# A decoder layer on one core: the second half's x is split before it is turned, and turned by transposing DMAs

## The reference, cut to what matters

```python
def _L0_attn_ref(u, ...):                       # u = x, axes l (16), b (256), d (512)
    xn = _layernorm(u, ln_gamma, ln_beta)
    up = jnp.einsum('lbd,ed->lbe', xn, W_in) + b_in          # e: 3 * 512
    uc = short causal convolution over l, 3 taps, of up
    x0, x1, v = jnp.split(uc, 3, axis=1)
    v = v * x1
    y = long convolution of v over l with k, + v * conv_bias
    y = y * x0
    return jnp.einsum('bld,ed->ble', y, W_out)
x = _layernorm(x + _L0_attn_ref(x, ...))
```

## Time and profile before

| what | us |
|---|---|
| three runs, median (lowest to highest) | 1064.82 (1059.51 to 1065.6) |
| the profiled execution's own time | 1063.69 |
| its span, first to last instruction | 1061.9 |
| TensorE busy | 1006.2 (95%) |
| VectorE busy | 799.3 (75%) |
| ScalarE busy | 599.9 (56%) |
| GpSimd busy | 552.7 (52%) |
| first half's output steps on TensorE | 182.33 to 246.17 |
| second half's slots, steps, and the end of the part | 246.17 to about 459 |

### The profile page before, as it was taken

The page is one execution under the profiler, slowest core; times in us unless marked ns, Lnnn a source line. Parts: engine busy times, 40 slices in busy tenths (PEclk is TensorE's granted clock), DMA queues, the critical chain, the costliest instruction groups (busy, mean ns, idle before and its releaser), DMA issues.

```text
span 1061.9 us, 14827 instructions
## 1 busy us (share of the span) xinstructions
PE 1006.2 (95%) x4679; PEld 602.9 (57%) x4679; DVE 799.3 (75%) x1509; ACT 599.9 (56%) x728; POOL 552.7 (52%) x886
## 2 busy tenths in 40 slices
PE   3899999999999999978999999999999999999985
PEld 2455545544445555456666666666666666666641
DVE  7967975786475567657888888888888888888862
ACT  5655544112566558114666666767576767676664
POOL 5320310221000004269787887878787878787861
PEclk9999999999999999989999999999999999999998
DMA  9323655456475777441444544444444444444334
GB/s 322 61 60 120 203 152 163 145 165 194 162 227 189 241 259 255 141 143 51 105 98 113 105 113 108 115 106 117 104 117 105 109 114 101 122 99 114 76 64 91
DMA packets 178220, 144.65 MB, mean 136 GB/s; under 512 B 99988, under 2 KB 132792, under 8 KB 176120
## 3 DMA queue, kind: packets, MB, share of 16 engines
q1 hardware_dynamic: 178168, 144.00, 49.3%
HBM read 89.29 MB, written 33.70 MB: 116 GB/s over the span
## 4 chain that ended last, share of the span: by engine, by line
PE 50%; DVE 2%; POOL 1%; ACT 1%; DMA 1%; issue 1%; POOLq 0%; DVEq 0%; ACTq 0%
PE conv_bank L1398 28%; PE hq_bank L1421 9%; PE ff_bank L1442 5%; PE back_bank L1442 5%; PE back_bank L1412 1%; PE back_bank L1381 1%; PE ctx_bank L1369 1%; DMA hq_t<-hq_int 0%; POOL sum L1742 0%; DVE z L1607 0%; DVE g_max L1674 0%; POOL sum L1744 0%; ACT g L1546 0%; DMA xq_t<-xq_int 0%; ACT hq_f L1507 0%
## 5 line engine op out<-in xcount | busy, mean ns | idle before, releaser
L1742 POOL TENSOR_TENSOR sum<-z 128x640 f32<-128x640 f32 x128 | 198.2, 1549 | 11.6 <-DVE z L1619 9.6
L837 DVE SCALAR_TENSOR_TENSOR conv_all<-u,taps,conv_all 128x1024 f32<-128x1024 f32 x92 | 122.4, 1331 | 93.2 <-ACT conv_all L708 91.4
L1398 PE MATMUL conv_bank<-block_diag 128*128 128x288 f32 x628 | 167.8, 411 | 1.8 <-DVE z L1619 1.8
L1398 PE MATMUL conv_bank<-kv,block_diag 128*128 128x288 f32 x640 | 168.6, 406 | 0.9 <-DVE z L1619 0.8
L1398 PEld LDWEIGHTS conv_bank<-kv,block_diag 128*128 128x128 f32 x640 | 117.8, 190 | 31.6 <-DVE z L1619 1.8
L1398 PEld LDWEIGHTS conv_bank<-block_diag 128*128 128x128 f32 x628 | 117.3, 193 | 32.4 <-DVE z L1619 2.2
L1421 PE MATMUL hq_bank<-x_lo,hq_t 128*128 128x512 f16 x512 | 122.2, 382 | 4.7 <-DMA hq_t<-hq_int 4.7
L1674 DVE TENSOR_REDUCE g_max<-g 128x1 f32<-128x512 f32 x128 | 85.8, 673 | 41.5 <-ACT g L1546 41.5
L700 ACT ACTIVATE u<-slot_bank,bias,unscale 128x1024 f32<-128x1024 f32 x46 | 55.4, 1204 | 108.9 <-PE slot_bank L509 88.6
L1744 POOL TENSOR_TENSOR sum<-sum 128x320 f32<-128x320 f32 x128 | 111.3, 869 | 10.0
L1607 DVE TENSOR_TENSOR z<-conv_bank,qx 128x512 f32<-128x512 f32 x128 | 88.0, 687 | 34.2 <-PE conv_bank L1398 24.6
(11 more groups left out here) (181 smaller groups left out, 1676.2 us busy)
## 6 DMA issues: line engine op xcount, KB each, us to landing
x_quad<-in_w SPq DMA_DIRECT2D x10, 1024.0 KB, 8.3
v_scratch<-conv_all SPq DMA_DIRECT2D x16, 512.0 KB, 3.5
c_scratch<-v_tok SPq DMA_DIRECT2D x8, 1024.0 KB, 5.3
y<-c_scratch SPq DMA_DIRECT2D x8, 1024.0 KB, 4.9
res<-in_x SPq DMA_DIRECT2D x32, 256.0 KB, 2.9
x_scratch<-res SPq DMA_DIRECT2D x32, 256.0 KB, 3.1
block_diag<-in_ctx SPq DMA_DIRECT2D x32, 256.0 KB, 3.7
block_diag<-ssm_scratch SPq DMA_DIRECT2D x32, 256.0 KB, 3.7
```

The source lines that it names most:

```text
L837: ins = nc.vector.scalar_tensor_tensor(out=acc, in0=(u_first[kind] if n < 3 else u)[:, t0 + tap:t0 + tap + T // 2, :].rearrange("p t b -> ...
L1398: last = nc.tensor.matmul(view(conv_bank[tb % 2][:, hh, :], 0, (ROW64, T // 2), (1, PAIRS)), toep[:, head.buf, (tb - sb_) * P:(tb - sb_ + ...
L1742: nc.gpsimd.tensor_tensor(sum2[:, :, :], z[:, b, :, 0:half], z[:, b, :, half:2 * half], ALU.add).then_inc(sum2_done, 1)
```

## The change

For the second half only, TensorE's 64 transposes (with 16 ScalarE copies and 16 VectorE subtractions out of PSUM) go. In their place, ScalarE casts a normalized quad to its float16 high part (`make_hi`, 128x2048 in one instruction), VectorE subtracts it from the quad to a float16 rest (`make_lo`, likewise), both still with the batch on the partitions and in an order of (block of 128 features, time, feature). The two lie side by side in a tile that is free by then (`conv[X1]`, `conv[V]`, `v_tok`, `conv[X0]` for quads 0 to 3). SyncE then issues two transposing DMAs a quad (`turn_halves`), each of 128x2048 float16, which write `x_hi` and `x_lo`, whose layout is now quad by quad. Slots 0 and 1 wait for these DMAs. `make_hi` stands after slots 20 and 23 for quads 0 and 1 and after the slots for quads 2 and 3; `make_lo` after slot 22 and in output steps 2, 9 and 12; the transposing DMAs behind the stores of output steps 0, 4, 10 and 13. The loads of x into `x_quad` wait for `make_lo` in place of the transposes. The first half works as before.

```diff
+        half_rows = [view(tile, 0, (1, T * P)).bitcast(F16) for tile in (conv[X1], conv[V], v_tok[:, :], conv[X0])]
+        def token_half(q, low):
+            return view(half_rows[q], low * QUAD * D, (1, QUAD * D))
+        def by_chunk(ap, step_dc, step_t):
+            return view(ap, 0, (step_dc, DC), (step_t, QUAD), (1, P))
...
-        QUAD_AT = {1: 0, 4: 1, 9: 2, 13: 3}
+        HI_AT = {20: 0, 23: 1}
+        LO_AT = {22: 0}
+        LATE_LO_AT = {2: 1, 9: 2, 12: 3}
+        TURN_X_AT = {0: 0, 4: 1, 10: 2, 13: 3}
...
@@ load_quad (SyncE)
-                        sp.wait_ge(x_turned, DC * (Q - 1))
+                        sp.wait_ge(lo_made, Q - NQ - 1)
...
+                def turn_halves(q):
+                    if q == 0:
+                        sp.wait_ge(slot_full, NSLOT)
+                    for low, (made, x) in enumerate(((hi_made, x_hi), (lo_made, x_lo))):
+                        sp.wait_ge(made, q + 1)
+                        sp.dma_start_transpose(view(x[:, q, :, :], 0, (P, DC * QUAD), (1, P)), token_half(q, low)).then_inc(halves_turned[q], 16)
...
                         store_res(R)
+                        if hf + 1 < HALF and t in TURN_X_AT:
+                            turn_halves(TURN_X_AT[t])
                         if hf + 1 < HALF and t in LOAD_QUAD_AT:
...
@@ slot (TensorE)
-                        elif hf > 0 and s < 2 and j < 2:
-                            pe.wait_ge(made, DC * (NQ * hf + 2 * (s + 1)))
+                        elif hf > 0 and s < 2 and j == 0:
+                            for q in group:
+                                pe.wait_ge(halves_turned[2 * pr + q], 2 * 16)
...
-                        if hf + 1 < HALF and t in QUAD_AT:
-                            turn_quad(NQ * (hf + 1) + QUAD_AT[t])
...
+                def make_hi(q):                                  # ScalarE
+                    act.wait_ge(x_normed, q + 1)
+                    if q == 0:
+                        act.wait_ge(vx_done, 2 * DC)
+                    elif q == 1:
+                        act.wait_ge(v_stored, 2 * 16 * DC)
+                    elif q == 2:
+                        act.wait_ge(c_stored, 16 * DC)
+                    else:
+                        act.wait_ge(y_done, 4 * DC)
+                    src = quad_buf(NQ + q)[:, :, :].rearrange("p t d -> p (t d)")
+                    nc.scalar.copy(by_chunk(token_half(q, 0), QUAD * P, P), by_chunk(src, P, D)).then_inc(hi_made, 1)
...
+                def make_lo(q):                                  # VectorE
+                    dve.wait_ge(hi_made, q + 1)
+                    src = quad_buf(NQ + q)[:, :, :].rearrange("p t d -> p (t d)")
+                    hi, lo = (by_chunk(token_half(q, low), QUAD * P, P) for low in range(2))
+                    nc.vector.tensor_tensor(lo, by_chunk(src, P, D), hi, ALU.subtract).then_inc(lo_made, 1)
...
-                        if more and t in QUAD_AT:
-                            split_lo(nxt + QUAD_AT[t])
+                        if more and t in LATE_LO_AT:
+                            make_lo(LATE_LO_AT[t])
```

More of the change, by code:

```diff
@@ L88, in hyena_block @@
         shift = sb("shift", [P, NQ, QUAD])
-        x_hi, x_lo = w["x_hi"], w["x_lo"]
+        x_hi, x_lo = (view(w[name][:, :, :], 0, (DC * QUAD * P, NQ), (QUAD * P, DC), (1, QUAD * P)) for name in ("x_hi", "x_lo"))
         u = sb("u", [P, T + TAPS - 1, P])
@@ L144, in hyena_block @@
         x_lo_done = sem("x_lo_done")
+        hi_made = sem("hi_made")
+        lo_made = sem("lo_made")
+        halves_turned = [sem(f"halves_turned{q}") for q in range(NQ)]
         u_zeroed = sem("u_zeroed")
@@ L457, in _ @@
             def _(pe):
[L458 to L464, removed]
                 def turn_quad(Q):
@@ L512, in slot, with convolve @@
                         last.then_inc(slot_full, 1)
-                def convolve(hf, cc, others=(), quad=None):
+                def convolve(hf, cc, others=()):
                     first = chain_counts(hf, cc)
@@ L521, in convolve @@
                     for k in range(4):
-                        if quad is not None:
-                            pe.wait_ge(x_lo_done, DC * quad + k + 1)
-                        elif not others:
+                        if not others:
                             pe.wait_ge(ch_copied, first - 4 + k + 1)
@@ L639, in _ @@
                         for cc in pieces_after(s):
-                            others, quad = (), None
+                            others = ()
                             if hf == 0 and cc < DC - 1:
                                 others = [(w_lo_done, KINDS * (cc + 2))] + [(wout_done, DC)] * (cc == 0)
-                            elif hf > 0 and cc == 0:
-                                quad = NQ * (hf + 1) - 1
                             if hf == 0 and cc == 0:
@@ L650, in _ @@
                                 pe.wait_ge(mean_made, 1)
-                            convolve(hf, cc, others, quad)
+                            convolve(hf, cc, others)
                     for t in range(PARTIAL):
@@ L784, in _ @@
                             copy_conv(hf, cc)
+                        if hf == 0 and s in HI_AT:
+                            make_hi(HI_AT[s])
                         if hf + 1 == HALF and s in SQUARE_AT:
@@ L789, in _ @@
                     if hf + 1 < HALF:
-                        for q in range(NQ):
-                            split_hi(NQ * (hf + 1) + q)
+                        make_hi(2)
+                        make_hi(3)
                 for i in range(2 * PARTS):
@@ L1001, in _ @@
                             norm_quad(nxt + QUAD_NORM_AT[s])
+                        if more and s in LO_AT:
+                            make_lo(LO_AT[s])
                         if not more and s == TOTAL_AT:
```

18 lines of the change are left out of this document (6 added, 12 removed).

## The result

The changed kernel took 1077.08 us (median of 4 runs, 1076.14 to 1078.82), the kernel before 1064.99 in the same runs: a ratio of 1.012, 95% interval 1.0089 to 1.015. The change costs 12.1 us. The forecast was 1085, the range 1068 to 1098: right in sign and mechanism, with the size overestimated by two thirds. The 1077 lies inside the forecast's own narrower range (1077 to 1093) only at its very edge.

The account below looks back on a forecast made before the run. TensorE was busiest, but SyncE's loop of landing, load and store was taken to have no slack. Slot 4 +17.8 us and clock +2.7 gave 20.5 us on 1063.69, 1084.2, stated as 1085; range 1068 to 1098.

Parts of the forecast that it names:

- The removal is worth nothing by itself: SyncE's output-step loop: a turn takes about 3.45 us, as much as TensorE's step, despite 8.8 us of removed TensorE work.
- The casts and subtractions are free: Four ScalarE casts and four VectorE subtractions: all eight taken at nothing; at most the first pair costs 1.9 + 2.5 us.
- A half takes 3.4 us of the transfer engines: Each 512 KB transposing transfer occupies all 16 engines 3.4 us, from 153 GB/s; bounds 2.8 us and 5 us.
- rival 4: Transposes slower beside loads: at 5 us a half, slot 4 about +32, total 1098 with the clock's share; chance 0.16.
- Rival 3: A transpose as fast as a plain transfer: 1.6 us a half, slot 4 at +4.7, total 1068; chance 0.05.
- 2.5 us of SyncE for a pair: SyncE's queue: issuing one pair of transposing transfers holds SyncE 2.5 us, from 1.25 us for one issue.
- The loop, step by step: SyncE's loop: pairs behind steps 0, 4 and 10 delay it by +4.3, +9.7 and +13.7 us.
- The last pair sets slot 1: Second half's slot 1 waits for step 13's pair: starts at 271.5 in place of 251.35.
- The weights' load behind the loop no longer shows by itself: Before slot 4: this load, behind the last pair, frees slot 4 at 286.9, against 287.0 from slot 1; earlier stall 2.14 us.
- The clock, +2.7: TensorE after idling 11 us before slot 1: granted clock at half costs 2.7 us; bounds 0 and twice that.
- Nothing gives it back: Behind slot 4: no delay is recovered, TensorE's waits there all being under 2 us until the second part.
- Rival 1: Only the wait on the last pair costs, the loop keeps its times: slot 4 +4.1, total 1068; chance 0.15.

Follow-up runs that it names:

- Experiment 1: Changed kernel without its eight transposing transfers and the second half's waits for them, so no transposes at all: 1064.2 us, ratio 0.9981 to the kernel before.
- experiment 4: Changed kernel with all eight transposing transfers issued by ScalarE in place of SyncE, each once its subtraction is done: 1073.5 us, ratio 1.0072.
- experiment 2: Changed kernel without the transposing pairs of output steps 0 and 4 and the wait for them: 1070.3 us, ratio 1.0053.
- experiment 3: Changed kernel with the last transposing pair behind the store of output step 12 in place of 13: 1073.7 us, ratio 1.0082.
- experiment 10: Changed kernel with 64 unread fill matmuls on TensorE between slots 0 and 1 of the second half: 1078.7 us, ratio 1.014.
- experiment 8: Changed kernel with stores first, quad loads, statistics, normalization and subtractions moved earlier, pairs behind steps 1, 3, 6 and 9: 1063.2 us, ratio 0.9983.
- experiment 11: As experiment 8, but each pair's two transposes put behind two neighbouring steps in place of one: 1052.7 us, ratio 0.989.
- (5): Changed kernel with one swap in SyncE's loop, the step's store issued before the residual load: 1074.9 us, ratio 1.0101.
- (12): Changed kernel with each pair's second transpose moved behind the next step's store, loads still first: 1076.0 us, ratio 1.0097.

## Why the prediction was right, and where its sizes were off

- **The removal is worth nothing by itself** ("this loop has no slack to give"): right, and stronger than I put it. Experiment 1 shows 8.8 us of TensorE's work gone and 0.3 us between the medians, at most 4 by the interval.
- **The casts and subtractions are free:** right. A cast took 1.9 us, a subtraction 2.29 us, and experiment 1, which keeps them, is no slower than the kernel before.
- **A half takes 3.4 us of the transfer engines:** this term was mis-sized, the main miss. I took the row of 153 GB/s, of a transfer of half the size. Landings of the three sizes say 187 GB/s, 2.8 us a half, the value that I had kept as the fast bound; the stretch in which a half moves alone says 219 GB/s, 2.4 us. The same walk with 2.8 us gives +12.8 us to slot 4 (the prediction's "+14" was a slip, and so was rival 4's "about +32", which comes to +30.5), with the clock 15.5, against 14.6 measured: this one term is 5.0 of the 8.3 us by which the sum was too high. The figure of the Trainium skill, page "Advanced Engine Details and Errata", section X-Bar Transpose (TRN2), an expected 350 to 400 GB/s, is not reached here. Rival 3, which stood on a transfer that fast, is out: at 1.6 us a half a landing would take some 3.4 us, and none was under 4.3.
- **2.5 us of SyncE for a pair:** wrong, it is 4.7 to 5.9. No cost of it by itself is seen: experiment 4 frees SyncE of it and the loop is hardly shorter.
- **The loop, step by step:** forecast +4.3, +9.7, +13.7 at the loads at 203.69, 227.14 and 244.91; measured, with the 2.1 us of the later start taken off, +3.1, +4.9 and +8.5. The pairs' data explain 3.9 of the last gap of 5.2 us: from the first half's issue to the second's landing the three took 7.0, 8.1 and 7.0 us in place of 8.65. The rest came in by step 7: I let the second load of 1 MB wait behind the whole pair and cost its 6 us again. SyncE was held so long by the pair (219.80 to 225.71) that its data were nearly through when that load was issued at 227.04; this is read from the trace and was not tested.
- **The last pair sets slot 1:** right. Forecast 8.6 us from issue to release, measured 7.8; forecast slot 1 at +20.2, measured +14.2 (267.67 less 2.1, against 251.35). That the wait before slot 1 came out as forecast, 11.25 us against 11, is luck: slot 0 ended 3.7 us earlier than the 260 that I had, and the landing came as much earlier. Experiments 2 and 3 move it as said.
- **The weights' load behind the loop no longer shows by itself:** right, slot 4 has no wait.
- **The clock, +2.7:** slot 1 took 2.67 us longer. Right in size within this trace; experiment 10 ties it to the idleness, but no total shows it, and other slots behind standstills paid between 1.3 us (experiment 3) and 2.9 us (experiment 8).
- **Nothing gives it back:** wrong by 2.4 of 14.6 us, 1.4 of them at the start of the second part, which I had not looked at.

Rival 1, the last pair alone, is refuted by the loop's +8.6 us and by experiment 2. In sum: forecast 17.8 + 2.7 = 20.5 us up to slot 4; measured 14.6 with the clock's 2.7 in it, less the 2.4, 12.2 us.

What stays open is why two transposes in a row cost experiment 8 more than one in each of two steps. The 10.6 us between the two stretches are accounted for: TensorE stands still 10.4 us in experiment 8 and 3.0 in experiment 11, and experiment 8's slow slot 0 adds 2.9. The cause of the late residual loads behind them is not shown. The data are the same, and taking the issues off SyncE in experiment 4 changed its loop little, though ScalarE issued the transposes in an order of its own there. What is shown: stores first without splitting (5) and splitting without stores first (12) each do little at the old positions; with early loads, early pairs and stores first, the splitting takes the time from 1063 to 1053. Splitting with early loads but loads first was not run, so whether the stores must go first is open.

## What to carry to other kernels

Before moving work off the busiest engine, look for a serial loop of waits on a queue beside it: here "wait for a landing, load, store" took 3.45 us a turn against TensorE's 3.47, and a 95% busy TensorE hid that it was not the only bound. Test it by leaving the work out altogether; that costs one run and says what the move can bring at most while the loop stays as it is (experiment 11, which changed the loop too, brought more). A loop that must absorb bursts needs turns that can be shorter than the average one (issue the store before the wait that belongs to the next load), and here it helped only once the bursts were also cut into pieces of about a turn and finished early.

## What I had not expected of the hardware

- A transposing DMA of 128x2048 float16 (512 KB) issued by SyncE lands in 4.3 to 6.1 us, was seen to move its data at 219 GB/s where nothing else moved, and holds SyncE 1.9 to 4.0 us; of 128x1024 it holds it 1.25 us, of 128x512 1.21 us (medians). The hold is not proportional to the size.
- Issued by ScalarE while SyncE loads and stores, transposes slow the loop about as much as in SyncE's own queue (59.05 us with five inside it, 59.95 with six), and one of ScalarE's issues was itself held 10 us while a 1 MB load of SyncE's took 11.1 us in place of 4.8.
- After 11.25 us of idleness TensorE's clock stood at half and the slot behind it took 7.85 us in place of 5.18; with the gap filled by 44 matmuls up to 3.5 us before the slot, it still took 6.86. Two standstills of 11.25 us cost the slot behind them 2.7 and 1.9 us, one of 5.83 us cost 2.9, and one of 2.14 us (before, slot 4) nothing.
